# A LoRA and routed-FFN kernel: another order of splits and pieces between fold and tiles, four left banks, late x tiles

## What is computed

```python
result = x + cond @ W_base.T + b_base          # W_base 512x512
probs  = softmax(cond @ W_gate.T)              # 8 experts
top_p, top_i = top_k(probs, 2); top_p /= sum(top_p)
h      = einsum('bnd,erd->bner', cond, A)      # 8 experts, rank 16
result += einsum('bner,eor->bno', h * route_w[..., None], B)
```

## Time and profile before

| | us |
|---|---|
| median of 3 runs (70.53 to 71.6) | 71.22 |
| the profiled execution | 71.81 |
| its span, first to last instruction | 70.1 |
| TensorE matmul busy (424) | 63.3 |
| TensorE weight load busy | 61.1 |
| VectorE busy (130) | 35.2 |
| ScalarE busy (76) | 26.8 |
| GpSimd busy (36) | 12.5 |

### The profile page before, as it was taken

How to read it: one execution, slowest core, us unless ns; L and a number is a source line. 1 busy time by engine, 2 the same in 40 slices (tenths; PEclk the granted TensorE clock), 3 DMA queues, 4 the chain that set the end, 5 groups by cost and what they waited for, 6 DMA issues and landing times.

```text
span 70.1 us, 1284 instructions
## 1 busy us (share of the span) xinstructions
PE 63.3 (90%) x424; PEld 61.1 (87%) x424; DVE 35.2 (50%) x130; ACT 26.8 (38%) x76; POOL 12.5 (18%) x36
## 2 busy tenths in 40 slices
PE   3999999999999953999599999999999999999850
PEld 3979999999999933999498999999999999999630
DVE  0033898001997996055806473663863633435420
ACT  5272893005938581011263343523711412323220
POOL 1002998400095030030004003003011000000000
PEclk9999999999999999559999999999999999999997
DMA  0899999993000002555404030030030030120304
GB/s 0 264 262 347 389 396 405 409 390 150 0 13 1 0 0 64 126 142 136 101 0 154 9 124 26 0 150 5 0 150 0 0 150 9 58 91 0 141 8 150
DMA packets 4648, 8.45 MB, mean 121 GB/s; under 512 B 793, under 2 KB 1049, under 8 KB 4642
## 3 DMA queue, kind: packets, MB, share of 16 engines
q1 hardware_dynamic: 4178, 7.70, 32.0%
q0 software_dynamic: 320, 0.54, 2.1%
q10 hardware_dynamic: 144, 0.13, 0.5%
HBM read 5.26 MB, written 2.10 MB: 105 GB/s over the span
## 4 chain that ended last, share of the span: by engine, by line
PE 50%; DVE 16%; DMA 8%; issue 8%; POOLq 7%; ACT 5%; POOL 2%; ACTq 0%; DVEq 0%
PE bank L451 15%; PE bank L452 14%; PE bank L453 14%; DMA lora_raw<-lora 8%; POOLq L211 6%; DVE x_lo L332 3%; DVE cl_lo L332 3%; PE bank L504 2%; POOL lora_raw L214 2%; PE bank L491 2%; PE bank L506 1%; DVE bw_lo L332 1%; PE bank L515 1%; DVE lb_lo L332 1%; DVE cr_lo L332 1%
## 5 line engine op out<-in xcount | busy, mean ns | idle before, releaser
L451 PE MATMUL bank<-cl_hi,x_hi 128*128 128x408 f32 x32 | 11.6, 363 | 0.0
L453 PE MATMUL bank<-cl_hi,x_lo 128*128 128x408 f32 x32 | 11.5, 360 | 0.0
L452 PE MATMUL bank<-cl_lo,x_hi 128*128 128x408 f32 x32 | 11.5, 359 | 0.0
L451 PE MATMUL bank<-cr_hi,x_hi 128*128 128x256 f32 x32 | 10.4, 325 | 0.0
L452 PE MATMUL bank<-cr_lo,x_hi 128*128 128x256 f32 x32 | 9.3, 290 | 0.0
L453 PE MATMUL bank<-cr_hi,x_lo 128*128 128x256 f32 x32 | 9.2, 287 | 0.0
L239 POOL CAST cl_hi<-lora_raw 128x64 fp32r<-128x64 f32 x8 | 2.7, 340 | 26.7 <-PE bank L453 26.6
L451 PEld LDWEIGHTS bank<-cr_hi,x_hi 128*128 128x128 f32 x32 | 6.5, 202 | 0.3
L332 DVE TENSOR_TENSOR x_lo<-x_raw,x_hi 128x512 fp32r<-128x512 f32 x8 | 5.2, 682 | 2.5 <-ACT x_hi L260 2.5
L452 PEld LDWEIGHTS bank<-cr_lo,x_hi 128*128 128x128 f32 x32 | 6.4, 199 | 0.0
L453 PEld LDWEIGHTS bank<-cl_hi,x_lo 128*128 128x128 f32 x32 | 6.3, 197 | 0.0
(11 more groups left out here) (90 smaller groups left out, 153.1 us busy)
## 6 DMA issues: line engine op xcount, KB each, us to landing
x_raw<-x_t SPq DMA_DIRECT2D x8, 256.0 KB, 6.7
out<-y_out SPq DMA_DIRECT2D x7, 256.0 KB, 2.0
w_raw<-fold_in SPq DMA_DIRECT2D x4, 324.0 KB, 5.0
w_raw<-fold_in SPq DMA_DIRECT2D x4, 256.0 KB, 5.2
bw_rows<-bw_hi SPq DMA_DIRECT2D x8, 81.0 KB, 2.1
lora_raw<-lora POOLq DMA_DIRECT2D x8, 64.0 KB, 5.0
bw_rows<-bw_lo SPq DMA_DIRECT2D x4, 81.0 KB, 2.1
ffn_b_raw<-ffn_b SPq DMA_DIRECT2D x1, 256.0 KB, 8.2
```

Of the source, the lines that this page charges most:

```text
L451: nc.tensor.matmul(out, a_hi, b_hi, start=first, stop=False, skip_group_check=True)
L452: nc.tensor.matmul(out, a_hi, b_lo, start=False, stop=False, skip_group_check=True)
L453: return nc.tensor.matmul(out, a_lo, b_hi, start=False, stop=last, skip_group_check=True)
```

## The change

- SP: chunk 0 of the fold's weights comes as columns 384 to 648 (`w_first_loaded`), then columns 0 to 384, then the rest, three DMAs for two. x tiles 0 and 1, `ffn_b` and bias follow the weights; x tiles 2 to 7 are issued only after all eight gathers have landed (`lora_loaded`).
- ScalarE and VectorE: x tiles 0 and 1 are split before `lb`; `ffn_b` is split right behind `lb`, ahead of the fold's banks; x tile 2 behind `cr`, x tile 3 behind `bw`. GpSimd splits the bias itself. In the first tiles ScalarE's order of copies is another, and x tile 4 is split ahead of the second `split_hw`.
- One Exp on a column of constants is ScalarE's first instruction; the warm-up matmuls read a constant in place of a zeroed tile.
- TensorE: Left uses four banks in turn (the fourth is bank 7). The pieces of tiles 0 to 2 come in another order, Lora(0) behind Right(0), whose first matmul now opens the bank. In tile 7 Lora stands ahead of the last chunk of Right(6), T2(7) comes two chunks earlier in Right(7), and Last_delta does its four hi matmuls before it waits for `hw_lo`. The first float32 products of chunk 0 begin with block 3.

```diff
@@ -27,6 +27,7 @@
 ROWS = ONES + 2
+FIRST = D - P
 WARM_UPS = 24
@@ -88,23 +89,23 @@
         y_out = sb("y_out", [P, NT, D])
-        zeros = sb("zeros", [P, P // 2])
+        table_warm = sb("table_warm", [P, 1])
         ident = sb("ident", [P, P])
...
         bank = [ctx.enter_context(nc.psum_tensor(f"bank{i}", [P, 512], F32)) for i in range(8)]
-        left_bank = bank[0:3]
+        left_bank = bank[0:3] + bank[7:8]
         right_bank = bank[4:6]
...
+        w_first_loaded = sem("w_first_loaded")
         wa_loaded = [sem(f"wa_loaded{m}") for m in range(KC)]
...
         lora_loaded, ffn_b_loaded, bias_loaded = sem("lora_loaded"), sem("ffn_b_loaded"), sem("bias_loaded")
-        zeros_ready = sem("zeros_ready")
         ident_zero, ident_ready, const_ready, pads_ready = (
@@ -159,7 +160,7 @@
         def left(t):
-            return left_bank[t % 3]
+            return left_bank[t % 4]
@@ -176,13 +177,24 @@
         def _(sp):
-            for m in range(KC):
+            sp.dma_start(w_raw[:, 0, FIRST:D + GH], fold_in[0, :, FIRST:D + GH]).then_inc(w_first_loaded, DMA)
+            sp.dma_start(w_raw[:, 0, 0:FIRST], fold_in[0, :, 0:FIRST]).then_inc(wa_loaded[0], DMA)
+            sp.dma_start(w_raw[:, 0, D + GH:], fold_in[0, :, D + GH:]).then_inc(wb_loaded[0], DMA)
+            for m in range(1, KC):
                 sp.dma_start(w_raw[:, m, 0:D + GH], fold_in[m, :, 0:D + GH]).then_inc(wa_loaded[m], DMA)
                 sp.dma_start(w_raw[:, m, D + GH:], fold_in[m, :, D + GH:]).then_inc(wb_loaded[m], DMA)
+            def load_x(t):
+                sp.dma_start(x_raw[:, t], x_t[t]).then_inc(x_loaded[t], DMA)
+            load_x(0)
+            load_x(1)
+            sp.dma_start(ffn_b_raw[:], ffn_b).then_inc(ffn_b_loaded, DMA)
             sp.dma_start(bias_raw[:], bias).then_inc(bias_loaded, DMA)
-            for t in range(NT):
-                sp.dma_start(x_raw[:, t], x_t[t]).then_inc(x_loaded[t], DMA)
-            sp.dma_start(ffn_b_raw[:], ffn_b).then_inc(ffn_b_loaded, DMA)
+            sp.wait_ge(lora_loaded, NT * DMA)
+            for t in range(2, NT):
+                load_x(t)
@@ -226,7 +238,10 @@
+            pool.wait_ge(bias_loaded, DMA)
+            nc.gpsimd.tensor_copy(bias_hi[:], bias_raw[:]).then_inc(bias_hi_done, 1)
             pool.wait_ge(bias_hi_done, 1)
+            nc.gpsimd.tensor_tensor(bias_lo[:], bias_raw[:], bias_hi[:].bitcast(F32), ALU.subtract).then_inc(bias_lo_done, 1)
             pool.wait_ge(bias_lo_done, 1)
@@ -244,23 +259,25 @@
         def _(act):
+            nc.scalar.activation(table_warm[:], nc.const_aps.tensor(0.0, [P, 1], F32), ACT.Exp)
+            act.wait_ge(w_first_loaded, DMA)
             for m in range(KC):
...
             nc.scalar.copy(wg_hi[:, 0, 0:GH], raw_gh(0)).then_inc(gh0_hi_done, 1)
-            act.wait_ge(lora_loaded, NT * DMA)
-            nc.scalar.copy(by_batch(lb_hi), raw_lb()).then_inc(lb_hi_done, 1)
-            act.wait_ge(bias_loaded, DMA)
-            nc.scalar.copy(bias_hi[:], bias_raw[:]).then_inc(bias_hi_done, 1)
...
-            for t in range(X_EARLY):
-                split_x(t)
+            split_x(0)
+            split_x(1)
+            act.wait_ge(lora_loaded, NT * DMA)
+            nc.scalar.copy(by_batch(lb_hi), raw_lb()).then_inc(lb_hi_done, 1)
+            act.wait_ge(ffn_b_loaded, DMA)
+            nc.scalar.copy(ffn_b_hi[:], ffn_b_raw[:]).then_inc(ffn_b_hi_done, 1)
@@ -272,11 +289,11 @@
                 nc.scalar.copy(cr_hi[:, 2 * n:2 * n + 2, :].rearrange("p c n -> p (c n)"), bank[4 + n][:]).then_inc(cr_hi_done, 1)
-            act.wait_ge(ffn_b_loaded, DMA)
-            nc.scalar.copy(ffn_b_hi[:], ffn_b_raw[:]).then_inc(ffn_b_hi_done, 1)
+            split_x(2)
             act.wait_ge(bw_summed, 1)
...
             nc.scalar.copy(bw_hi[:, LEFT:], bwr_bank[:, 0:HALF]).then_inc(bw_hi_done, 1)
+            split_x(3)
@@ -304,16 +321,18 @@
             copy_xa_t(0)
+            copy_xa_t(1)
             exp_top(0)
-            copy_xa_t(1)
+            split_hw(0)
             exp_top(1)
-            split_hw(0)
+            split_x(X_EARLY)
+            split_hw(1)
+            copy_xa_t(2)
             copy_left(0)
             copy_right(0)
-            split_x(X_EARLY)
-            split_hw(1)
             for t in range(2, NT):
-                copy_xa_t(t)
+                if t >= 3:
+                    copy_xa_t(t)
                 exp_top(t)
@@ -338,17 +355,17 @@
             lo(wg_lo[:, 0, 0:GH], raw_gh(0), wg_hi[:, 0, 0:GH], gh0_lo_done)
-            dve.wait_ge(lb_hi_done, 1)
-            lo(by_batch(lb_lo), raw_lb(), by_batch(lb_hi), lb_lo_done)
-            dve.wait_ge(bias_hi_done, 1)
-            lo(bias_lo[:], bias_raw[:], bias_hi[:], bias_lo_done)
...
-            for t in range(X_EARLY):
-                split_x(t)
+            split_x(0)
+            split_x(1)
+            dve.wait_ge(lb_hi_done, 1)
+            lo(by_batch(lb_lo), raw_lb(), by_batch(lb_hi), lb_lo_done)
+            dve.wait_ge(ffn_b_hi_done, 1)
+            lo(ffn_b_lo[:], ffn_b_raw[:], ffn_b_hi[:], ffn_b_lo_done)
@@ -374,12 +391,12 @@
-            dve.wait_ge(ffn_b_hi_done, 1)
-            lo(ffn_b_lo[:], ffn_b_raw[:], ffn_b_hi[:], ffn_b_lo_done)
+            split_x(2)
             dve.wait_ge(bw_hi_done, 1)
...
             lo(bw_lo[:, LEFT:], bwr_bank[:, 0:HALF], bw_hi[:, LEFT:], bw_lo_done)
+            split_x(3)
@@ -432,8 +449,8 @@
             split_hw(0)
+            split_xa(2)
             split_x(X_EARLY)
-            split_xa(2)
             split_hw(1)
@@ -462,11 +479,10 @@
             def Left(t, chunks):
-                if t >= X_EARLY - 1 or chunks[0] == 0:
-                    pe.wait_ge(x_lo_done, t + 1)
+                pe.wait_ge(x_lo_done, t + 1)
                 pe.wait_ge(la_lo_done, t + 1)
-                if t >= 3:
-                    pe.wait_ge(yl_done, t - 2)
+                if t >= 4:
+                    pe.wait_ge(yl_done, t - 3)
                 for c in chunks:
@@ -479,7 +495,8 @@
                         pe.wait_ge(cr_lo_done, c // 2 + 1)
-                    product(right(t), x_hi[:, t, c, :], x_lo[:, t, c, :], cr_hi[:, c, :], cr_lo[:, c, :], False, False)
+                    product(right(t), x_hi[:, t, c, :], x_lo[:, t, c, :], cr_hi[:, c, :], cr_lo[:, c, :],
+                            t == 0 and c == 0, False)
@@ -504,7 +520,7 @@
                 nc.tensor.matmul(right(t), xa_t[0:ROWS, t % 2, :], bw_rows[:, t // 2, LEFT:],
-                                 start=True, stop=False, skip_group_check=True).then_inc(lz_done, 1)
+                                 start=(t > 0), stop=False, skip_group_check=True).then_inc(lz_done, 1)
@@ -523,13 +539,25 @@
-            pe.wait_ge(zeros_ready, 1)
+            def Last_delta():
+                t = NT - 1
+                halves = ((left(t)[:, OUT_LEFT], slice(0, HALF), zl_done), (right(t), slice(HALF, D), zr_done))
+                pe.wait_ge(hw_hi_done, t + 1)
+                for z, cols, _ in halves:
+                    nc.tensor.matmul(z, hw_hi[:, t % 2, :], ffn_b_hi[:, cols], start=False, stop=False, skip_group_check=True)
+                    nc.tensor.matmul(z, hw_hi[:, t % 2, :], ffn_b_lo[:, cols], start=False, stop=False, skip_group_check=True)
+                pe.wait_ge(hw_lo_done, t + 1)
+                for z, cols, done in halves:
+                    nc.tensor.matmul(z, hw_lo[:, t % 2, :], ffn_b_hi[:, cols], start=False, stop=True, skip_group_check=True).then_inc(done, 1)
+            ones = nc.const_aps.tensor(1.0, [P, P], mybir.dt.bfloat16)
             for _ in range(WARM_UPS):
-                nc.tensor.matmul(bwr_bank[:, 0:P], zeros[:].bitcast(mybir.dt.bfloat16), zeros[:].bitcast(mybir.dt.bfloat16),
-                                 start=True, stop=True)
-            pe.wait_ge(wa_loaded[0], DMA)
-            for i in range(KC):
+                nc.tensor.matmul(bwr_bank[:, 0:P], ones, ones, start=True, stop=True)
+            pe.wait_ge(w_first_loaded, DMA)
+            for i in (3, 0, 1, 2):
+                if i == 0:
+                    pe.wait_ge(wa_loaded[0], DMA)
                 nc.tensor.matmul(bank[i][:, 0:GH], w_raw[:, 0, i * P:(i + 1) * P], raw_gh(0),
@@ -560,33 +588,47 @@
             Left(0, (0, 1, 2, 3))
...
             Left(1, (1, 2, 3))
-            Lora(0)
             Right(0, (0, 1))
...
             Right(0, (2, 3))
+            Lora(0)
             Lora(1)
+            Left(2, (0, 1, 2))
             T2(0)
-            Left(2, (0, 1))
+            Left(2, (3,))
+            Right(1, (0, 1, 2, 3))
             Delta(0)
-            Left(2, (2, 3))
             T2(1)
-            for t in range(2, NT):
+            T1(2)
+            Left(3, (0, 1))
+            Lora(2)
+            Delta(1)
+            Left(3, (2, 3))
+            T2(2)
+            for t in range(3, NT - 1):
                 Right(t - 1, (0, 1))
...
                 Delta(t - 1)
-                if t + 1 < NT:
```

(21 more changed lines are left out.)

## The result

| | before | after |
|---|---|---|
| median of 4 runs beside each other | 71.31 us | 68.16 us |
| range of these runs | 70.53 to 71.6 | 67.92 to 68.22 |
| the profiled execution, its span | 71.81, 70.1 | 67.92, 66.2 |

The ratio is 0.958 with a 95% interval of 0.951 to 0.965. Ratios with an interval leave out the slowest executions of each kernel, so they are not the quotients of the medians beside them. The change makes the kernel 3.15 us faster by the medians, 3.9 us by the two profiled executions. The forecast was 66.9 with a range of 65.8 to 68.8: right in sign and range, 1.26 us too low. Beside other runs of before the gain was 3.87 (71.64 to 67.77) and 3.09 (71.10 to 68.01), so it is itself not one number. Why is the main thing that this study shows.

What follows compares the result with a forecast made beforehand. It took TensorE's waits on VectorE's queue, headed by the LoRA gathers, and the following low clock as the bound. 2.0 + 1.65 + 0.7 + 0.24 - 0.2 - 0.35 + 0.45 - 0.2 = 4.3, so 71.22 becomes 66.9 us, range 65.8 to 68.8.

Steps and rivals of the forecast that it cites:

- The hole: TensorE's 2.1 us idle before T1(0), waiting for VectorE's xa_rows: would go, gain 2.0 us.
- part 1: Order of splits and transfers on SP, ScalarE, VectorE, GpSimd: T1(0) at 25.5 rather than 27.47, gain 2.0 us.
- the six late x tiles: x tiles issued on SP after the gathers: the gathers, no longer sharing the engines with them, would land between 13 and 16.6.
- The clock: TensorE's low-clock stretch 28.30 to 31.80, behind the idle time: would not come, gain 1.65 us, bounds 0 and 1.75.
- The pieces: TensorE order in tiles 0 to 3: gains 0.7 at Delta(0), 0.24 at T1(2); losses 0.2 at Lora(2), 0.35 at T1(3).
- The end: Tile 7: Lora(7) 0.18 us earlier, 0.33 wait for hw_lo avoided; gain 0.45 us, bounds 0.2 and 0.6.
- The front: First weights in one more piece: an extra issue delays the fold's start, loss 0.2 us, bounds 0 and 0.46.
- (a): Rival: TensorE's low clock comes all the same, after short stalls or a different early ramp; 68.6 us, chance 0.13.
- (b): Rival: x tiles 2 or 3 land late, so T1(0) still waits 1.2 us; 68.1 to 69.7 us, chance 0.06.
- (c): Rival: slower, x tile 2 landing so late that idle time and low clock return in full; about 72.7 us, chance 0.02.
- (d): Rival: no change, VectorE's queue not the cause since TensorE's own work fills the time; 71.2 us, chance 0.04.

Runs made afterwards that it cites:

- splits_only: Kernel before with only the new order of splits on ScalarE, VectorE, GpSimd and the late x tiles: 68.11 us beside 71.77, ratio 0.965.
- x_at_once: Changed kernel without SP's wait for the gathers, x tiles 2 to 7 issued right behind bias: 67.97 us beside 67.77 of the changed kernel.
- filled_hole: Kernel before with ten extra matmuls, result thrown away, in TensorE's idle time before T1(0): 70.84 us beside 71.77.
- pieces_only: Kernel before with only the new order of pieces in the tiles, four left banks and the new last delta: 71.15 us beside 71.77.
- splits_again: Second run of the kernel before with only the new split order and late x tiles: 68.65 us, beside 71.10 before and 68.01 changed.
- old_end: Changed kernel with the last tile's old order and the plain Delta(7) put back: 68.30 us beside 67.77 of the changed kernel.
- three_two_queues: Changed kernel with ScalarE issuing chunk 0's second half and, at tile 2, split_xa(3) ahead of split_x(5): 67.62 us beside 68.01 of the changed kernel.
- one_piece: Changed kernel with chunk 0's weights in two DMAs again: median 67.59 us of four executions (two left out) beside 67.77 of the changed kernel.

## Why the prediction was right, and what was off

**The hole.** Right: 1.94 us of it went (2.0 in the sum), for the reason given, and splits_only shows that part 1 alone does it. The part of that step that says the six late x tiles help is not borne out in the changed kernel (x_at_once is the same); with the old front it is open. `cl_lo` started at 17.56, as forecast; the gathers' wait ended at 14.39 and not near 13.5, and `wg_hi` ended at 5.70 and not by 5.6. Neither mattered.

**The clock.** The mechanism is right and shown from both sides (filled_hole: hole filled, no fall in 12; pieces_only: hole left, fall in 5 of 6). The term of the sum is what was mis-sized, twice. 1.65 us was taken off a median as if every execution had the low stretch; by the granted clocks 21 of 39 have it. And it costs 1.14 in one that has it (1.10 by the timelines): 3.5 us at 0.51 were counted as half lost, but the matmuls there are 0.34 us apart in place of 0.19, not twice, and 0.3 us covered the wait of Lora(0). The last sentence of the sum, which carries the whole 4.3 from the execution with 71.81 over to the median of 71.22, is the step that failed. The sign of the trouble was in the runs shown: 70.53 to 71.6 with a profiled one at 71.81 is a wide spread for one kernel, and the prediction called it scatter.

**The sum without the fall.** Against executions of before that have no fall, the table of stretches gives 2.07 (the hole, 22.19 to 20.12), 0.39 (18.47 to 18.08, mostly the wait at Lora(0)), 0.68 (the pieces) and 0.30 (the end): 3.44 us. Measured, chip by chip, are 3.32 (71.09 to 67.77) and 2.95 (70.96 to 68.01), so the front takes back 0.1 to 0.5. The prediction's own terms, with 0.3 for the wait at Lora(0) in place of the clock's 1.65, give 2.95 too, but with the pieces too small, the end too large and the front at 0.2: that this is the measured number is in part luck.

**The pieces.** Delta(0) lost its wait, T1(2) too; T1(3) waits 0.28 (0.35 in the sum); Lora(2) 0.1 (0.2 in the sum: 35.80 against 35.52 + 0.19 in the timeline). The four terms add up to 0.39; the timelines have 0.68, of which 0.67 comes under the low clock as well. Which of the pieces has the 0.3 more was not taken apart. Splits_again puts the pieces, the end and the front together at 0.64 by its medians, the same as the sum's terms, but with a scatter of 1.3 us that agreement says little.

**The end.** 0.45 forecast; 0.30 by the timelines of old_end, 0.53 by its medians. Lora(7) does wait 0.17 for `xa_t`, as said.

**The front.** 0.2 forecast. In the profiles `wg_hi` starts at 4.65 to 5.79 with three pieces (5 kernels, middle 5.08) and at 4.33 to 4.77 with two (7 kernels, middle 4.50). The middle is 0.58 later, with more scatter than that inside the first kind; in five of the seven `wg_hi` did not wait for its transfer at all. Of this little reaches T1(0): it starts at 25.87 to 26.58 with three pieces (5 kernels) and at 25.34 to 26.21 with two and no hole (4 kernels). One reason stands in the timelines: the float32 products end between 5.1 and 6.3, according to how long the low level lasts, and hold the fold back in their own right in some executions. What the third piece costs stays open, between nothing and 0.5 us.

**Rivals.** (a) did not come: no low slice behind the front in any kernel without the hole, but for the last one, after the work. (b) and (c) need x2 late; x_hi(2) never waited for its transfer. The landing in (b) is a slip (16.6 + 6.7 is 23.3, not 23.8), without effect. (d) is out.

## What to carry to other kernels

Before an expected saving is subtracted from a median, ask whether the profiled execution has something that the others may lack; the granted clock of every execution is a one-line test. A wait of TensorE can cost twice, once as a hole and once as clock, and filling it with thrown-away matmuls separates the two in one run. Put work whose input comes late (here the gathers' splits) behind work that is ready, and place what is needed last (x tiles 2 and 3) into the gaps. Before an order of transfers is called useful, undo it alone: here it was worth nothing in the final kernel. Where medians scatter by more than the effect, distances between landmarks inside the timelines can still tell it.

## What the runs showed of the hardware

A hole of 2.1 us on TensorE was followed by a low stretch in 21 of 39 executions by their mean granted clock, not always and not never. The wait of 0.67 us at Delta(0) in filled_hole was followed by none in 12, the 0.5 to 0.6 us there in splits_only and splits_again by none in 13.

At the front the granted clock column reads 1.00 from the start of the span, but the spacing of the matmuls does not. In the low stretch of before, products of 256 columns start 0.21 us apart, elsewhere 0.12. In the profile of three_two_queues:

```profile
6.32 0.41 PE L480 MATMUL bank<-wg_hi,wt_hi 128*128 128x256 f32 x1
6.53 0.41 PE L478 MATMUL bank<-wg_hi,wt_hi 128*128 128x256 f32 x1
...
9.04 0.28 PE L478 MATMUL bank<-wg_hi,wt_lo 128*128 128x256 f32 x1
9.16 0.28 PE L480 MATMUL bank<-wg_hi,wt_lo 128*128 128x256 f32 x1
```

They are 0.21 us apart until 8.9 and 0.12 from 9.04 on, while the column has 1.00 for 0:3, 3:6 and 6:9 alike. The eight float32 matmuls took 1.19 us (one_piece) to 2.50 us (three_two_queues) for the same reason. So the low level lasts into the fold in some executions, and the column is not to be trusted at the front.

VectorE's and GpSimd's work met where both read SBUF: `lb_lo` took 1.10 us beside GpSimd's `bias_lo` (13.99 to 15.59) and 0.69 without it. The Trainium skill says so ("SBUF — State Buffer", section "Who interferes with whom": a VectorE instruction with two SBUF inputs contends with a GpSimd instruction that reads SBUF), and this trace agrees. In seven profiles `lb_lo` started 0.27 to 1.23 us before `bias_lo` was through; it lasted 0.82 to 1.78 us there and ended 0.55 us after the end of `bias_lo` each time, whatever its start. That is what waiting for `bias_lo` looks like, not slower work side by side. It cost nothing, since `cl_lo` had to wait for `cl_hi` behind the fold.

With the small first transfer the gathers were issued from 5.56 to 5.61 us (5 kernels), with the large one from 6.37 to 7.11 (7 kernels): GpSimd reads the adapter indices before them, while the weights are being transferred. In three_two_queues, where the small first transfer has ScalarE's half beside it, they were issued at 7.06, so the size of the first transfer alone does not decide it. That is an association over thirteen profiles; no run was made for it.
